# Scan stage of a four-layer block on one core: one and a half feed-forward halves per slot, decays in SBUF, low parts on GpSimd

## The reference

```python
x = x + _L0_xattn_ref(_layernorm(x), fside, ctx)          # int8-rounded gate/up/down linear layers, per batch
x = x + _L0_ffn_ref(_layernorm(x), lut, gate_idx, ...)    # weights = lut[idx]: silu(x Wg) * (x Wu) @ Wd, inner width 1376
x = x + _L1_xattn_ref(ctx, _layernorm(x), ...)            # state space scan over 512 steps
x = x + _L1_ffn_ref(_layernorm(x), ...)                   # 32 experts, 8 per token
```

```python
def step(state, inp):
    d, b, c, u = inp
    dA = jnp.exp(d[..., None] * A)
    state = state * dA + (d * u)[..., None] * b[:, None, :]
    y = jnp.einsum('bdn,bn->bd', state, c)
    return (state, y)
y = y + D[None, :, None] * x
y = y * silu(z)          # z is the layer-normalised x, so it follows the second layer
```

## Time and profile before

| | us |
|---|---|
| median of 3 runs (lowest to highest) | 1888.23 (1886.31 to 1891.99) |
| the profiled execution's own time | 1889.96 |
| its span | 1888.2 |
| front stage, 0 to about 533 | 533 |
| scan stage, about 533 to 1178 | 645 |
| last products and expert stage, to the end | 710 |

### The profile page before, as it was taken

One profiled execution on the slowest core, in us unless ns is written; L12 is line 12 of the kernel. 1 busy time (PEld: TensorE's weight loads), 2 busy tenths in 40 slices (PEclk: granted clock), 3 DMA queues, 4 the chain that ended last, 5 costly groups with the idle time before them and its releaser, 6 DMA issues. The chain is left out here.

```text
span 1888.2 us, 26253 instructions
## 1 busy us (share of the span) xinstructions
PE 1535.6 (81%) x9320; PEld 1311.2 (69%) x9328; DVE 1311.7 (69%) x1918; ACT 910.4 (48%) x1579; POOL 794.1 (42%) x477
## 2 busy tenths in 40 slices
PE   5858778676528987996898799647899999999895
PEld 3445355454428976895797699646789998989785
DVE  6677586786569999999999998624445555555452
ACT  3444546445234444345444444414556666666563
POOL 1010000010054456446555553367735766762555
PEclk9878788887759988997998899859999999999998
DMA  7988799985582591384369146359999999999875
GB/s 211 342 282 269 279 322 369 334 270 170 182 312 106 180 350 62 127 301 192 107 229 345 62 143 232 152 213 341 385 360 232 252 265 253 260 252 232 214 171 76
DMA packets 187941, 445.46 MB, mean 236 GB/s; under 512 B 41616, under 2 KB 43664, under 8 KB 177568
## 3 DMA queue, kind: packets, MB, share of 16 engines
q1 hardware_dynamic: 115040, 283.37, 44.3%
q0 software_dynamic: 31760, 74.48, 16.8%
q10 hardware_dynamic: 41008, 85.89, 12.6%
HBM read 246.77 MB, written 205.28 MB: 239 GB/s over the span
## 5 line engine op out<-in xcount | busy, mean ns | idle before, releaser
L1438 POOL TENSOR_TENSOR mix_st<-mix_Bb,mix_du 128x2048 f32<-128x2048 f32 x64 | 293.4, 4584 | 268.0 <-DVE mix_st L2158 255.5
L2150 DVE TENSOR_TENSOR_SCAN mix_st<-mix_YY,mix_st 128x512 f32<-128x512 f32 x256 | 311.7, 1218 | 46.6 <-POOL mix_st L1438 24.2
L1856 ACT ACTIVATE mix_YY<-mix_dt,mix_A 128x512 f32<-128x512 f32 x256 | 176.9, 691 | 275.0 <-DVE mix_st L2150 270.9
L1482 POOL DMA_INDIRECT out_x<-moe_ys,moe_meta x130 | 211.6, 1628 | 192.7 <-ACT moe_ys L1982 82.0
L1603 PE MATMUL mix_G<-mix_xThi,mix_wup 128*128 128x256 f32 x1408 | 271.4, 290 | 15.8 <-issue 14.9
L1603 PEld LDWEIGHTS mix_G<-mix_xThi,mix_wup 128*128 128x128 f32 x1408 | 230.3, 198 | 18.9 <-issue 17.5
L1764 PE MATMUL mix_Dp<-moe_xhi,moe_whi 128*128 128x288 f32 x768 | 233.4, 304 | 0.9 <-DVE moe_wlo L2254 0.8
L1764 PE MATMUL mix_Dp<-moe_xlo,moe_whi 128*128 128x288 f32 x768 | 227.5, 296 | 0.0
L1764 PE MATMUL mix_Dp<-moe_xhi,moe_wlo 128*128 128x288 f32 x768 | 227.5, 296 | 0.0
L1629 PE MATMUL mix_YY<-mix_ident,mix_st 128*128 128x128 f32 x1024 | 144.7, 296 | 89.7 <-DVE mix_st L2158 89.7
L2264 DVE TENSOR_TENSOR moe_xlo<-mix_G,moe_xhi 128x512 fp32r<-128x512 f32 (+1 forms) x160 | 102.0, 638 | 164.5 <-ACT moe_xhi L1945 161.4
(11 more groups left out here) (216 smaller groups left out, 3059.8 us busy)
## 6 DMA issues: line engine op xcount, KB each, us to landing
x_by_expert<-front_zeros ACTq DMA_DIRECT2D x16, 4480.0 KB, 23.4
mix_wup<-w_halves SPq DMA_DIRECT2D x44, 1024.0 KB, 5.6
moe_raw<-in_ew SPq DMA_DIRECT2D x32, 1280.0 KB, 8.3
moe_xt<-x_by_expert SPq DMA_DIRECT2D x128, 256.0 KB, 8.5
mix_wdn<-w_halves SPq DMA_DIRECT2D x44, 512.0 KB, 6.4
front_idx<-in_idx SPq DMA_DIRECT2D x44, 384.0 KB, 8.9
w_halves<-front_wst SPq DMA_DIRECT2D x44, 384.0 KB, 7.8
mix_Bb<-bc_rows SPq DMA_DIRECT2D x16, 1024.0 KB, 9.6
```

The costliest lines, as they stand in the source:

```text
L1438: nc.gpsimd.tensor_tensor(st[:, g % STBUF, :, :], Bb[:, q, :, :], du[:, k % 2, :].unsqueeze(1).to_broadcast([P, NG, S]), ALU.mult).then_in ...
L1482: pool.indirect_dma_start(out=out_rows, out_offset=bass.IndirectOffsetOnAxis(ap=meta[0:rows, e % MBUF, j, 0:1].bitcast(U32), axis=0), in_= ...
L1856: nc.scalar.activation(dA, dt[:, k % 2, :], ACT.Exp, scale=A[:, c, m:m + 1]).then_inc(da_ready, 1)
L2150: nc.vector.tensor_tensor_scan(r, dA, r, 0.0, ALU.mult, ALU.add).then_inc(scanned, 1)
```

## The change

- `ups_of_slot` replaces the table: `up` starts in slot 1 of a batch, and each slot has one and a half halves (36 matmuls); `down` is dealt out in steps of one token tile, three a slot, through `DOWNS`.
- `dA` becomes two SBUF buffers. A decay waits for the scan before the last, and is made two scans ahead.
- The freed bank of `YY`, named `stage`, takes two of the four transposed row groups of the next batch (slot 0) and, in turn, the four transposed groups of z (slots 6 and 7); the other two row groups go through `G` (`T`).
- `low_half` moves from VectorE to GpSimd, behind `inputs_product`. `hidden` waits for it before it overwrites `hf`.
- Statistics of the next batch's rows move to slot 12 of the batch before, `normalise` to slot 14, transposes, high and low parts to slot 0; for the first batch they stand ahead of the first scan. The statistics of the third sum move to slot 10.
- `u` has one buffer instead of two, which makes room; it is loaded in the first slot of its channel group and scaled in the third.

```diff
+def ups_of_slot(g):
+    b, l = divmod(g, UNITS)
+    if g < 0 or b >= NB or l == 0:
+        return []
+    k = 3 * ((l - 1) // 2)
+    if l == UNITS - 1:
+        own = [(k, (0, 1))]
+    elif l % 2 == 1:
+        own = [(k, (0, 1)), (k + 1, (0,))]
+    else:
+        own = [(k + 1, (1,)), (k + 2, (0, 1))]
+    return [(HALVES * b + i, vs) for i, vs in own]
...
 def halves_of_slot(g):
-    if g < 0 or b >= NB or l < FIRST_SLOT:
-        return []
-    done = sum(1 if k in ONE_IN else 2 for k in range(FIRST_SLOT, l))
-    return [HALVES * b + done + k for k in range(1 if l in ONE_IN else 2)]
+    return [i for i, vs in ups_of_slot(g) if 1 in vs]
...
+def downs_by_slot():
+    slots, ready = [], []
+    for g in range(NB * UNITS + 3):
+        ready += [(i, t) for i in halves_of_slot(g - 2) for t in range(HT)]
+        n = len(ready) if g > NB * UNITS else DOWN_STEPS
+        slots.append(ready[:n])
+        ready = ready[n:]
+    return slots
...
+        dA = few("dA", [P, 2, S], F32)
...
-        u = sb("u", [P, 2, S], F32)
+        u = sb("u", [P, S], F32)
...
-        dA = YY[:, 0, :]
+        stage = YY[:, 0, :]
...
+        def rows_bank(c):
+            return stage if c in (0, DC - 1) else T[:, c - 1, :]
+        def z_bank(b, t):
+            return stage if b < NB - 1 else Dp[:, t, :]
...
             load_b(0, 0)
+            load_x(0)
             load_c(0, 0)
-            load_x(0)
...
+            def low_half(i):
+                pool.wait_ge(hhi_ready, i + 1)
+                if i >= HBUF:
+                    pool.wait_ge(half_done, i - HBUF + 1)
+                nc.gpsimd.tensor_tensor(hlo[:, i % HBUF, :], hf[:, i % 2, :], hhi[:, i % HBUF, :].bitcast(F32),
+                                        ALU.subtract).then_inc(hlo_ready, 1)
...
                 if g < ALL - 1:
                     inputs_product(g + 1)
+                for i in halves_of_slot(g - 1):
+                    low_half(i)
                 if l in (4, 5) and b > 0:
                     for t in range(HT):
                         z_by_tanh(b - 1, (l - 4) * HT + t)
...
+                if l == 0 and b < NB:
+                    for c in range(DC - 1):
+                        rows_transposes(b, c)
+                if l == Z_SLOT and has_z:
+                    z_transposes(b - 1, 0)
+                for i, t in DOWNS[g]:
+                    down(i, t)
+                if l == 0 and b < NB:
+                    rows_transposes(b, DC - 1)
+                if l == Z_SLOT + 1 and has_z:
+                    z_transposes(b - 1, 2)
+                for i, vs in ups_of_slot(g):
+                    up(i, vs)
                 if g < ALL:
                     sum_states(g, 0)
+                if l == Z_SLOT and has_z:
+                    z_transposes(b - 1, 1)
+                if l == Z_SLOT + 1 and has_z:
+                    z_transposes(b - 1, 3)
...
-                if step > 0:
-                    act.wait_ge(scanned, step)
+                if step > 1:
+                    act.wait_ge(scanned, step - 1)
-                nc.scalar.activation(dA, dt[:, k % 2, :], ACT.Exp, scale=A[:, c, m:m + 1]).then_inc(da_ready, 1)
+                nc.scalar.activation(dA[:, step % 2, :], dt[:, k % 2, :], ACT.Exp, scale=A[:, c, m:m + 1]).then_inc(da_ready, 1)
...
+                if i > 1:
+                    dve.wait_ge(hlo_ready, i - 1)
                 nc.vector.scalar_tensor_tensor(out=hf[:, i % 2, :], in0=th[:, i % 2, :], scalar=0.5,
                                                in1=G[:, i % 2, 1, :], op0=ALU.mult, op1=ALU.mult).then_inc(h_ready, 1)
...
-                nc.vector.tensor_tensor_scan(r, dA, r, 0.0, ALU.mult, ALU.add).then_inc(scanned, 1)
+                nc.vector.tensor_tensor_scan(r, dA[:, step % 2, :], r, 0.0, ALU.mult, ALU.add).then_inc(scanned, 1)
...
             for g in range(ALL):
...
-                for i in formed:
-                    low_half(i)
```

More of the change, by code:

```diff
@@ L885 @@
 HALVES = 2 * CH
-FIRST_SLOT = 3
-ONE_IN = (3, 4, 6, 15)
 Z_SLOT = 6
+DOWN_STEPS = 3
 UPW = 2 * D
@@ L1077, in mix_and_experts_block @@
         dt_du_in = [sem(f"dt_du_in{i}") for i in range(2)]
-        u_in = [sem(f"u_in{i}") for i in range(2)]
+        u_in = sem("u_in")
         b_in = [sem(f"b_in{i}") for i in range(GROUPS)]
@@ L1312, in _ @@
                     downs += 1
+                if q == 0 and k > 0:
+                    load_u(b, c)
                 if l == 10:
@@ L1513, in _ @@
                     constants()
+            for i in halves_of_slot(ALL - 1):
+                low_half(i)
             pool.wait_ge(prod_ready, 2 * ALL)
@@ L1590, in up, with rows_transposes @@
-            def up(i):
+            def rows_transposes(b, c):
+                if c == 0:
+                    pe.wait_ge(norm_ready[0], TT * b + TT)
+                    if b > 1:
+                        pe.wait_ge(zT_read, TT * (b - 1))
+                elif c == DC - 1:
+                    pe.wait_ge(lo_ready, DC * b + 1)
+                elif b > 0:
+                    pe.wait_ge(h_ready, HALVES * b + c - 2)
+                for t in range(TT):
+                    last = nc.tensor.transpose(rows_bank(c)[:, t * P:(t + 1) * P], xn[:, t, c * P:(c + 1) * P], ident[:, :])
+                last.then_inc(xT_ready, 1)
@@ L1599, in up @@
                 cols = slice(half * HALF, (half + 1) * HALF)
-                for v in range(2):
+                for v in vs:
                     steps = [(c, x, part) for c in range(DC) for x, part in ((xThi, 0), (xTlo, 0), (xThi, 1))]
@@ L1604, in up, with down @@
                                                 x[:, c, cols], start=(n == 0), stop=(n == len(steps) - 1))
-                last.then_inc(gu_ready, 1)
-            def down(i):
+                if 1 in vs:
+                    last.then_inc(gu_ready, 1)
+            def down(i, t):
                 b, h = divmod(i, HALVES)
@@ L1610, in down @@
                 rows = P if h // 2 < CH - 1 else LAST
-                pe.wait_ge(dn_in[j % DNBUF], 16 * (j // DNBUF) + 16)
-                pe.wait_ge(hlo_ready, i + 1)
-                if h == 0 and b > 0:
-                    pe.wait_ge(yz_ready, b)
-                for t in range(HT):
-                    for n, (hid, part) in enumerate(((hhi, 0), (hhi, 1), (hlo, 0))):
-                        last = nc.tensor.matmul(Dp[:, half * HT + t, :], hid[0:rows, i % HBUF, t * P:(t + 1) * P],
-                                                wdn[0:rows, j % DNBUF, part, :],
-                                                start=(h // 2 == 0 and n == 0), stop=(h // 2 == CH - 1 and n == 2))
-                last.then_inc(half_done, 1)
+                if t == 0:
+                    pe.wait_ge(dn_in[j % DNBUF], 16 * (j // DNBUF) + 16)
+                    pe.wait_ge(hlo_ready, i + 1)
+                    if h == 0 and b > 0:
+                        pe.wait_ge(x2_ready, b)
+                for n, (hid, part) in enumerate(((hhi, 0), (hhi, 1), (hlo, 0))):
+                    last = nc.tensor.matmul(Dp[:, half * HT + t, :], hid[0:rows, i % HBUF, t * P:(t + 1) * P],
+                                            wdn[0:rows, j % DNBUF, part, :],
+                                            start=(h // 2 == 0 and n == 0), stop=(h // 2 == CH - 1 and n == 2))
+                if t == HT - 1:
+                    last.then_inc(half_done, 1)
             def sum_states(g, part):
@@ L1715, in _ @@
             ranks(0)
-            z_transposes(NB - 1)
+            for t in range(TT):
+                z_transposes(NB - 1, t)
             transposes_and_logits(2)
@@ L1992, in _ @@
             decay(0)
+            decay(1)
+            for t in range(TT):
+                normalise(0, 0, xt[:, 0, :, :], t)
             for g in range(ALL):
@@ L1998, in aside @@
                 def aside(t):
-                    if l == 1:
-                        normalise(0, b, xt[:, b % 2, :, :], t)
+                    if l == 0:
+                        rows_high(b, t)
+                    if l == 14 and b + 1 < NB:
+                        normalise(0, b + 1, xt[:, (b + 1) % 2, :, :], t)
                     if l == 3 and b > 0:
@@ L2010, in _ @@
                 aside(0)
-                decay(NG * g + 1)
+                decay(NG * g + 2)
                 for i in formed[1:]:
@@ L2024, in _ @@
                 aside(3)
-                decay(NG * g + 4)
-                if q == 1:
+                decay(NG * g + 5)
+                if q == 2:
                     skip_path(k)
-                if l == 2:
-                    for c in range(DC):
-                        rows_high(b, c)
             for i in halves_of_slot(ALL - 1):
@@ L2284, in inner_low, with next_rows @@
                 nc.vector.tensor_tensor(to, frm, hi.bitcast(F32), ALU.subtract).then_inc(e_hlo_ready, 1)
+            def next_rows(b):
+                return xt[:, (b + 1) % 2, :, :]
+            dve.wait_ge(x_in[0], 16)
+            moments(0, xt[:, 0, :, :], range(TT))
+            aggregate(0)
```

178 lines of the change are left out of this document (78 added, 100 removed).

## The result

The changed kernel takes 2086.15 us (median of 4 runs, 2080.08 to 2089.93); the kernel before, run beside it, 1890.1 us (4 runs, 1886.31 to 1891.99). The ratio is 1.104, interval 1.1011 to 1.107: slower by 196 us. The prediction was 2115, range 2010 to 2165.

What follows compares the result with a forecast made beforehand. It took VectorE as busiest in the scan stage, TensorE full in slots 9 to 14. Batches with full scan waits sum to 878 us, +234, giving 2122; best packing gives 2060; it took 2115, range 2010 to 2165.

Steps and rivals of the forecast that it cites:

- The row that decides: Scans with both operands in SBUF wait fully for GpSimd's 4.5 us input product, once a slot; 2115 with it, 1860 without.
- Step 1: `low_half` to GpSimd: VectorE loses 32.7 us of instructions, gains about 17 us in all; each takes 0.73 us on GpSimd.
- Step 2: Two decay buffers: VectorE's 21.9 us of waits for decays go.
- Step 3: One and a half halves per slot from slot 1: VectorE's 15.5 us of waits for tanh go.
- Step 4: Next batch's rows early: start costs 6.4 us, between nothing and 8; slot 0 waits about 1.7 us a batch.
- Step 5 and 6: z through one bank may cost 1.5 us a batch; u with one buffer is hidden, at worst 2 us a column.
- The sum: Scan stage with full waits: slots of 11.5, 12.15 and 13.7 us, total 878, ending at 1412 against 1178: +234.
- A: Rival: scans read decays without touching the shared path; stage ends at 1148, 30 us off, 1860; chance 0.11.
- B: Rival: scans free, but TensorE the bound; at 10 us a slot the stage is 646, time 1890; chance 0.03.
- C: Rival: partial exclusion, GpSimd's product interrupted, half of the wait; 2005, reach 1930 to 2050; chance 0.05.

Runs made afterwards that it cites:

- experiment 1: The kernel before with only the decay moved from a PSUM bank to one SBUF buffer, order and waits untouched: 2087.18 us, ratio 1.1052.
- experiment 2: The changed kernel with GpSimd's 64 input products replaced by fills that read nothing: 1888.19 us with zeros (3859.63 us with other constants, when overflow code ran).
- experiment 4: The changed kernel with GpSimd's input product cut to two of four states, the others filled with zeros: 1955.62 us, ratio 1.0353.
- experiment 8: The kernel before with `low_half` on GpSimd, up projections spread, and `hidden` split around scan 1 in slots with one half: 1875.71 us, ratio 0.9942.
- Experiment 7: The kernel before with `low_half` on GpSimd and the up projections spread more evenly over slots 3 to 15: 1880.52 us, ratio 0.9952.
- experiment 10: The changed kernel with GpSimd's input products replaced by fills with zeros and `low_half` back on VectorE: ratio 0.9868, which on 1889 us is 1864.
- experiment 6: The kernel before with only the 88 `low_half` moved to GpSimd, decays still in PSUM: 1888.01 us, ratio 0.9992.
- experiment 5: The changed kernel with one edit undone, the 88 `low_half` back on VectorE: 2067.95 us, ratio 1.0948.

## Why the prediction was right, and where its terms were off

**The row that decides: right, now shown.** It was an inference from two products to 256 scans; experiment 1 shows the decay's place by itself to cost what the change costs, experiment 2 that it is GpSimd's reading, experiment 4 that the cost follows the length of it. The handover 0.1 us before GpSimd's end held for scans too (0.12 and 0.13). The 2115 was 29 us too high, 15% of the change; that is a matter of the terms below. The Trainium skill (SBUF — State Buffer, Who interferes with whom) limits the conflict to GpSimd instructions that read, "not with one that only writes it"; the fills agree, with 1888 us. The same page of the Trainium skill (Summary: rules for kernel authors) has the second of the two to issue blocked until the first finishes; for two operands read the traces agree, to 0.12 us. With one operand read the scan's own time began 1.85 us before the end of GpSimd's record, so the measurement goes by less than the whole record there.

**Step 1, `low_half`: the mechanism right, the size too large.** Its own duration was estimated at 0.73 (the line through the two rows gives 0.74); where the scans leave it alone, in the version of experiment 8, the median is 0.742, and in the changed kernel, where it stands behind VectorE's work in its turn, 1.290. But the schedule charged VectorE the whole 0.73 for each. In the slot above product 0 takes 1.71 and not 1.20, scan 3 1.74 and not 1.22: 0.51 and 0.52. That is its 0.72 (the shortest of 88 is 724 ns) less the 0.12 of the early handover and less the 0.08 by which VectorE's operations overlap anyway; I had allowed for neither. This is most of what the prediction has too much: slots of 11.8 and 13.1 us against 12.15 and 13.7, over eight and seven of them 2.8 + 4.2 = 7.0 of the 8.5 us by which a batch is shorter (GpSimd's products of the second slot of batches 1 and 2 start at 726.78 and 941.27, 214.5 apart, against 223).

**Step 2, decays in two buffers: right.** No wait for one is left; with one buffer in SBUF, in experiment 1, there were 25.2 us.

**Step 3, one and a half halves a slot: right on waits, overvalued.** The wait for tanh went from 15.5 to 6.1, three waits at the starts of batches. Experiment 7 gives the even spread of TensorE's work, with `low_half` away, 8 us in the kernel before; in the changed one held scans set the pace, and what it gives there was not tried alone.

**Step 4, rows early: too low.** Scan 0 starts at 535.50 (533.7 predicted), scan 1 at 543.80 (541.8), the next slot at 552.00 (550.2), against 543.77: 8.2 us, just past the bound of 8, not 6.4. The 1.8 were there at scan 0: the statistics alone take 2.5 us, and the first scan stands behind them:

```profile
532.69 2.47 DVE L2180 BATCH_NORM_STATS2 mix_stats<-mix_xt 128x6 f32<-128x512 f32 x4 [22.13 <-DMA mix_xt<-x_store]
535.20 0.38 DVE L2185 BATCH_NORM_AGGREGATE mix_mv<-mix_stats 128x2 f32<-128x6 f32 x4
535.50 1.19 DVE L2203 TENSOR_TENSOR_SCAN mix_st<-mix_dA,mix_st 128x512 f32<-128x512 f32 x1
543.20 0.69 DVE L2224 TENSOR_TENSOR mix_xTlo<-mix_YY,mix_xThi 128x512 fp32r<-128x512 f32 x1 [6.51 <-ACT mix_xThi L1951]
```

In the later batches the rows cost (19.1 - 7.2) / 3 = 4.0 us of waiting and not 1.7. (The 7.2 are the first batch's, 6.51 and 0.69.)

**Step 5 and 6.** One bank for z was not tried alone. For u nobody waits, neither ScalarE nor TensorE.

**The sum.** The stage's end was put at 1412 and came at about 1378: three batches at 8.5 too long make 25.5; in batch 0 the same slots make 6 to 7, and the 1.8 of its start go the other way. That leaves some 4 us. Inside a batch the slots explain 7.0 of the 8.5, and the rows went 2.3 the other way, so nearly 4 us a batch of the other terms (statistics, z products, cover) were set too high and were not traced one by one.

**Rivals.** A's number, 1860, is nearly what experiment 10 shows, 1864, once its premise (nothing holds the scans) is made true; experiment 2 shows that with the input product alone out of the way 1888 would have come of it, because `low_half` and z read too. B does not appear: TensorE has 201.8 us of waiting for products. C was a reading of the mechanism, and only the operation with one operand read looks like it, at 2028.

TensorE's mean granted clock in the stage was 0.86 against 0.90, with TensorE busy for 620 of 847 us against 551 of 644. No slot shows a cost of it, since TensorE waits for VectorE's products in most of them (114 waits, 128 products).

## What to carry to other kernels

Before an operand of a VectorE instruction moves from PSUM to SBUF, count how many SBUF operands it then has, and what GpSimd reads beside it: if both overlap, their times add (here to within 0.13 us of an operation that reads two operands). Read it off the longest duration in a group whose median is unchanged, and find the other engine's end near the point where the operation's own time began. An operation taken off the busiest engine is worth its time only if no other engine is close behind (TensorE's 10.2 us of a 10.25 us slot in experiment 6), and if it doesn't come back as a hold (experiment 5).

## What the runs showed that was not expected

The whole of a ten per cent loss came from one line that names a buffer; everything else in a large change came out even beside it (2087 for the line alone, 2086 for all, 1888 for all without the product), and not because it did nothing: 19 us of gain and 18 of loss cancel (experiment 5). A GpSimd operation that reads one operand, with a record of 5.37 us at the least, let the scans in 1.85 us before the record's end, one that reads two 0.13 before it. A fill of 2048 elements on GpSimd takes 1.81 us and disturbs no scan. And to split the cover between two round trips gave nothing: through one decay buffer two scans start no closer than about 2 us (742.04, 744.08, 746.06 in experiment 8; the least of all is 1.97 there and in the kernel before, and 1.13 in the changed kernel with two buffers), so 0.4 us of other work between them hides 0.4 us of wait, wherever it is put.
